# Low parts of four experts' weights cut into 32 pieces of 64 columns, one behind every row transfer, on GpSimd

## What is computed

```python
xn = _layernorm(x, axis=-1)
x = x + _L0_attn_ref(xn, ...) + _L0_ffn_ref(xn, ...)
...
logits = x @ w_router.T
_, top_idx = jax.lax.top_k(logits, TOP_K)
mask = jax.nn.one_hot(top_idx, E, dtype=logits.dtype).sum(axis=1)
scores = jax.nn.sigmoid(logits) * mask
masked_inputs = scores.T[:, :, None] * x[None, :, :]
gate_up = jnp.einsum('eth,ehf->etf', masked_inputs, gate_up_proj)
gate, up = jnp.split(gate_up, 2, axis=-1)
expert_out = jnp.einsum('etf,efh->eth', up * jax.nn.silu(gate), down_proj)
shared = jax.nn.silu(x @ w_gate.T) * (x @ w_up.T) @ w_down.T
out = shared + expert_out.sum(axis=0)
```

## Time and profile before

| | us |
|---|---|
| median of 3 runs | 222.03 |
| the three runs | 221.5, 227.11, 222.03 |
| span of the profiled execution | 234.0 |
| PE busy in it | 211.0 (90%) |
| DVE, ACT, POOL busy | 151.4, 128.1, 135.0 |
| its mean granted TensorE clock | 0.977 |

### The profile page before, as it was taken

The page is one execution under the profiler, slowest core; times in us unless marked ns, Lnnn a source line. Parts: engine busy times, 40 slices in busy tenths (PEclk is TensorE's granted clock), DMA queues, the critical chain, the costliest instruction groups (busy, mean ns, idle before and its releaser), DMA issues.

```text
span 234.0 us, 4523 instructions
## 1 busy us (share of the span) xinstructions
PE 211.0 (90%) x1288; PEld 164.0 (70%) x1289; DVE 151.4 (65%) x361; ACT 128.1 (55%) x302; POOL 135.0 (58%) x214
## 2 busy tenths in 40 slices
PE   4999999999999997848999999899989998897894
PEld 4787888987875753436577797687777787784672
DVE  3977699788897785533663857556645456562871
ACT  2465868775577864343487445334433334582851
POOL 3573958800888888874020077787777787855400
PEclk9999999999999999985799999999999999999999
DMA  6999999950271271118205322123222231000993
GB/s 181 326 382 290 290 189 184 194 241 3 54 196 45 68 205 47 46 48 201 48 0 51 50 75 79 52 74 82 60 84 74 63 79 45 20 0 0 290 319 114
DMA packets 33334, 28.37 MB, mean 121 GB/s; under 512 B 8835, under 2 KB 29450, under 8 KB 32672
## 3 DMA queue, kind: packets, MB, share of 16 engines
q1 hardware_dynamic: 30784, 23.85, 41.1%
q0 software_dynamic: 2528, 4.24, 5.9%
HBM read 14.36 MB, written 10.50 MB: 106 GB/s over the span
## 4 chain that ended last, share of the span: by engine, by line
PE 76%; DVE 9%; issue 5%; another core or an unknown queue 3%; ACT 3%; POOL 2%; DMA 1%; DVEq 0%; ACTq 0%
PE acc L1512 10%; PE mid L1501 8%; PE mid L1362 7%; PE acc L1379 7%; PE big L1178 6%; PE big L1180 5%; PE acc L1235 5%; PE big L1179 5%; PE big L1346 4%; PE big L1343 4%; PE acc L1403 3%; DVE eht L873 3%; PE mid L1206 2%; PE acc L1197 2%
## 5 line engine op out<-in xcount | busy, mean ns | idle before, releaser
L482 POOL DMA_INDIRECT y_rows<-y,slot_info x47 | 47.0, 1001 | 25.4 <-ACT y L1137 15.3
L445 POOL DMA_INDIRECT scratch<-rows,slot x32 | 33.1, 1035 | 20.3 <-DVE slot L718 12.5
L772 DVE TENSOR_REDUCE negmax<-big 128x1 f32<-128x128 f32 (+7 forms) x32 | 24.1, 755 | 23.0 <-PE big L1346 15.3
L873 DVE COPY eht<-mid 128x512 f32<-128x512 f32 (+1 forms) x24 | 16.3, 680 | 27.1 <-PE mid L1501 24.8
L1059 ACT COPY pt<-mid 128x512 f32<-128x512 f32 (+3 forms) x48 | 22.1, 481 | 21.2 <-PE mid L1362 11.4
L1137 ACT COPY y<-acc 128x256 f32<-128x256 f32 (+1 forms) x24 | 8.8, 368 | 43.8 <-remote 20.4
L1512 PEld LDWEIGHTS acc<-wed,eht 128*128 128x128 f32 x188 | 23.5, 191 | 11.8 <-issue 10.8
L1512 PE MATMUL acc<-wed,eht 128*128 x188 | 26.2, 281 | 6.2 <-DVE eht L873 5.3
L1045 ACT ACTIVATE prob<-big,negmax 128x128 f32<-128x128 f32 (+7 forms) x32 | 23.7, 743 | 8.1 <-DVE negmax L772 6.2
L1362 PE MATMUL mid<-identf,prob 128*128 128x128 f32 x144 | 23.1, 285 | 4.9 <-issue 3.3
L1362 PEld LDWEIGHTS mid<-identf,prob 128*128 128x128 f32 x144 | 17.0, 144 | 10.5 <-issue 6.8
(11 more groups left out here) (144 smaller groups left out, 462.5 us busy)
## 6 DMA issues: line engine op xcount, KB each, us to landing
we_raw<-w_gate_up SPq DMA_DIRECT2D x4, 1024.0 KB, 10.1
scratch<-blank SPq DMA_DIRECT2D x1, 3120.0 KB, 27.3
xe<-scratch SPq DMA_DIRECT2D x24, 130.0 KB
q_raw<-qk_all SPq DMA_DIRECT2D x8, 256.0 KB
k_raw<-qk_all SPq DMA_DIRECT2D x8, 256.0 KB
wed<-w_down SPq DMA_DIRECT2D x1, 2048.0 KB, 31.4
expert_out<-y_rows SPq DMA_DIRECT2D x8, 256.0 KB, 4.7
out<-res SPq DMA_DIRECT2D x7, 256.0 KB, 3.4
```

What stands on the lines that cost most here:

```text
L445: pool.indirect_dma_start(scratch, bass.IndirectOffsetOnAxis(ap=slot[:, t:t + 1], axis=0), rows[:, t, :], None).then_inc(row_sent[t % FLY] ...
L482: pool.indirect_dma_start(y_rows, bass.IndirectOffsetOnAxis(ap=slot_info[:, t, 0:1].bitcast(U32), axis=0), y[p % NY][:, t % 2, :], None, b ...
L772: dve.tensor_reduce(negmax[:, i:i + 1], buf[:, at:at + (i + 1) * P], AX.X, ALU.max, negate=True).then_inc(max_ready, 1)
```

## The change

The pieces of POOL's low parts become half as wide and twice as many, and one stands behind each of the 32 row transfers. Nothing is left for behind the last one but its own piece. The sum of columns stays 2048, and PE's wait on `wel_ready` goes from 28 to 44. No other list changes.

```diff
                 pool.indirect_dma_start(scratch, bass.IndirectOffsetOnAxis(ap=slot[:, t:t + 1], axis=0),
                                         rows[:, t, :], None).then_inc(row_sent[t % FLY], 16)
-                if t % 2 and t // 2 < PIECES - BEHIND:
-                    weights_lo(t // 2)
-            for n in range(PIECES - BEHIND, PIECES):
-                weights_lo(n)
+                weights_lo(t)
...
-LOW_PIECE = 128
-PIECES = 16
-BEHIND = 4
+LOW_PIECE = 64
+PIECES = 32
```

## The result

| | median us | runs |
|---|---|---|
| before, same chip and day | 221.76 | 221.5, 227.11, 222.03, 220.5 |
| changed | 225.87 | 226.21, 225.52, 226.4, 225.44 |

The ratio is 1.0213, interval 1.0171 to 1.0254. Executions of one kernel fall into a faster and a slower group, and every ratio and interval here goes by the faster group alone, so it need not be the ratio of the medians beside it. The forecast was 222.0, with 224.5 as the upper end of its range. The profiled execution of the changed kernel has a span of 224.0 us, one of the four above; the one of before had 234.0, so the two spans can't be compared with each other.

A forecast was written before the change was run, and what follows sets the result against it. The prediction took the chain over PE, ACT and DVE as the bound, with PE busy for 90% of the span. Both terms, later rows and later end of POOL's stretch, were hidden: 222.0 us, unchanged, range 220.9 to 224.5.

The forecast's parts named there:

- Price of a piece: POOL: a 64-column subtraction takes 0.314 us and adds 0.23 us of pace, bounds 0.17 to 0.38.
- Where the last row transfer goes: POOL: the last transfer starts 2.5 us later, bounds 0.6 to 7.2, with 1.2 more possible from stretched pieces.
- The cover of 10.07 us: POOL's idle time ahead of line 453, waiting for PE, hides the stretch's end coming 1.1 us later; cost nothing.
- Waits on the weights: No piece waits for the high parts, and PE's wait on `wel_ready` keeps its last event; cost nothing.
- When the rows are there: SP's `xe` load: landed at about 113.9 us in the profiled execution, 111.9 in faster runs, before the change.
- The slack in the runs that count: PE at line 1321 in faster runs: arrives at 115.2, slack 3.3 us; the change takes 2.5, no cost, 0.8 spare.
- The rule of the skill: POOL and DVE share SBUF ports in turn; each of 16 additional piece starts may be held or hold DVE.
- (a): Rival at PE's first row read: slack gone in faster runs, delay passes one to one, 224.5 us; chance 0.23.
- (b): Rival on POOL: a 64-column piece costs about as much as a 128-column one, 225.9 to 227.1 us; chance 0.06.
- (c): Rival on DVE: the port holds fall on its instructions, about 0.5 us on the end, 222.5; chance 0.12.
- (d): Rival: pieces between eight close transfers remove the unexplained stop at 101 us, 7.5 us go, 214.5; chance 0.04.
- signs of being wrong: PE idle ahead of line 1321, pieces of 0.4 us or more, or the 101 us stop moving or vanishing with the time.

The follow-up runs named there:

- e0_before: The kernel before, without edit, profiled again on another chip: span 227.0 us, its median there 230.3 us.
- e1_all_behind: The kernel before with all 16 pieces behind the last row transfer: 257.64 us beside 230.27 for before, ratio 1.1352.
- e10_memsets: e1_all_behind with three one-column memsets behind every row transfer: 247.3 us beside 220.7 for before.
- e4_late_read: The changed kernel with PE's first two transposes of rows and ACT's high parts moved later: 223.93 us beside 228.13 for changed and 220.74 for before.
- e12_tiny_read: e1_all_behind with a one-column addition, which reads SBUF, behind every row transfer: 233.7 us (one run) beside 232.7 for before.
- e13_memsets10: e1_all_behind with ten one-column memsets behind every row transfer: 233.8 us (one run) beside 232.7 for before.
- e2_delay12: The kernel before with an idle 64-column addition behind each of the first 12 even transfers: 230.81 us beside 230.27 for before, ratio 1.0104.

## Why the prediction was wrong

**Price of a piece: right.** 0.33 us median against 0.314, pace 1.50 against 1.50.

**Where the last row transfer goes: right in its main term, short in the other.** Forecast 2.5 us later against the first, measured 51.1 - 46.9 = 4.2, inside the bounds of 0.6 to 8.4 (over all profiles of the two kernels 46.6 to 47.9 before, 51.1 to 53.0 changed). The 31 pieces at a pace of 0.24 give 31 x 0.24 - 4.6 = 2.8. The remainder of 1.4 is what the forecast priced at 1.2 us and left out of its sum: the pieces' mean is 0.387 against a median of 0.33, and some transfers are long themselves (1.95 us at 101.15). The stretch ends at 111.3, forecast 109.1. The cover of 10.07 us behind it is gone, because PE came early, but nobody waits for POOL there.

**Waits on the weights: right.** No wait of PE on `weh` or `wel`.

**When the rows are there: right by luck.** `xe` landed 2.2 us behind its issue. In e0_before that is 108.54 + 2.2 = 110.7 (forecast 111.9), in the changed kernel 114.3 (forecast 114.4): 3.6 us later, where 2.5 were forecast. A start 1.2 us too late and a shift 1.1 us too small cancel.

**The slack in the runs that count: the step that failed.** It put PE's arrival at 115.2 and took it to be the same in both kernels. As a figure for before it is near, though not for the forecast's reason: e0_before arrives at 115.67 with its clock never below 1.00, but it is not free of stops, since DVE's 2.0 us and ACT's 3.2 and 2.1 us stand ahead of it. The changed kernel has no such waits, and its PE arrives at 109.5, ahead of the rows in either kernel. The slack of 3.3 us was made of the very stops that the change removes. The rows became the bound, and the wait brought the lower clock with it, which the forecast didn't price at all: from the first transpose to the stage it is 127.9 - 114.29 = 13.6 us here and 125.5 - 115.67 = 9.8 in e0_before, 3.8 us more. It is 9.8 in all five profiles of before, and 13.4 to 14.0 in the three of the changed kernel.

An estimate from these rows shows how the two could make up the 4.1 us. With the clock up, rows at 110.7 and PE waiting for them, the stage would start at 110.7 + 9.8 = 120.5, and end the execution at 120.5 + 74.0 + 24.3 = 218.8 (24.3 is 226.2 - 201.9, the first changed profile's time less the stage's end); before's fastest run is 218.94. Before's median of 221.8 lies 3.0 above that, so with the same stage PE would start on the rows some 3 us later there, at 113.7, just before the changed kernel's rows come (114.3). The lateness of the rows then makes 0.6 us and the clock behind the new stop 3.8, together 4.4, which is 226.2 - 221.8. The 3.0 is fitted to before's median, so the sum must come out and bears nothing out; on the chip where before takes 220.7 and the changed kernel 228.1 it would be another. What is measured is that PE waits, that the work behind the wait takes 3.8 us longer, and that moving the reads back or the transfers out moves the time. The split is open: the five profiles of before have spans of 227.0 us and more and stages of 78 to 79 us, so no row here shows before with PE at 113.7 or a stage of 74.

**The rule of the skill.** The Trainium skill, page "SBUF — State Buffer", section "Who interferes with whom", lets a start of a piece be held by DVE's instructions. The trace agrees: the changed kernel's pieces stretch by 0.06 us in the mean, and all eight that take over 0.36 us start beside a two-input instruction or a cast of DVE. In the sum this would be up to 31 x 0.06 = 1.8 us more on the last transfer, by an estimate from these rows about what it lacked, so it deserved a term. It isn't what held PE's results up: e1_all_behind has no piece at all between its transfers and e10_memsets only memsets, which read nothing, and they have the most of such waits, 59.0 and 57.6 us.

**The rivals.** (a), the slack gone, came nearest, at a chance of 0.23. But it had the slack gone in before's faster runs already, and in no profile of before does PE wait for the rows; it is gone in the changed kernel, because PE comes sooner. Its price of 2.5 us left out the clock. (b) named the size (225.9) for a reason that the pieces refute. (c) is refuted: between 58 us and its first read of the rows PE stands still for 0.2 us in all, so no held DVE instruction reaches it. (d) was refused for a wrong reason: the stop at 101 us did lie with the eight close transfers, and in the changed kernel, with a piece between them, it is gone. That POOL's own pace doesn't change in a stop says nothing about what the transfers do to PE's results. What it gives back was lost again at the rows. Of the prediction's own signs of being wrong, two came: idle time ahead of line 1321, and the stop near 101 us vanished.

## What to carry to other kernels

A slack that is read from a slow execution may consist of the disturbance that makes it slow, and the disturbance may hide under more than one name in the trace: ask what it is in an execution of the median's length, and in the changed kernel, where the disturbance may be gone. Work put between transfers is paid in the arrival of the last one; if it is wanted for the spacing, the reader has to move back too, as in e4_late_read, which here brought no more than the loss back. And a wait that is new on TensorE is priced with the clock behind it, not by its own length alone.

## What the runs showed of the hardware

In this kernel, indirect transfers that GpSimd issues 1.27 us apart hold back what ACT and DVE get from PE, by up to 16.7 us at a time, though the DMA engines are 16% busy (e1_all_behind). Its unexplained waits on both engines are 59 us, against 9.3 at 1.37 (e12_tiny_read), and 4.8 and 0 at 1.5 (e13_memsets10, changed). It builds up: before, with 8 such transfers in a row, PE comes 6 to 15 us behind the changed kernel, and with 32 in a row 34 us.

What is held is open. The trace shows PE's matmuls as ended long before ACT may read them, but the Trainium skill, page "Perfetto Trace Analysis", section "Tensor Engine Instruction (MATMUL, LD_WEIGHTS)", calls the Tensor engine a special case that seems to have few profiling signals, so the rows can't tell a matmul that ran late from a signal that came late; no run here tells it either. Open, too, is why the expert stage takes 74 to 76 us on one chip and 79 on others.

A stop of 4.8 us without work on PE was followed by a granted clock of 0.50 until a little after 122 us, at a cost of 3.8 us on top of the stop. Short waits for the rows did not keep the clock up: behind the 1.7 us of e4_late_read it is 0.61 and 0.54 from 116 to 120, and behind the 0.9 us of e2_delay12, which has other gaps ahead of it, 0.62 and 0.53 from 114 to 118. In e0_before PE is busy for only 3.1 of the 6 us from 104 to 110, and it stays at 1.00.
